# One block for attention, output products, routing and experts: semaphores in place of two barriers

## What is computed

```python
qkv = (x @ Wqkv + bqkv).reshape(B, L, 3, n_heads, head_dim)      # B, L, D = 2, 2048, 256
scores = q . k / sqrt(head_dim) + slopes * -|pos_q - pos_k|
x = layernorm(x + softmax(scores) @ v @ Wout + bout)
weights = softmax(x @ router_w.T + router_b)                      # 4096 tokens, 8 experts
top two of each token; expert e takes its first 512 tokens
y = sum over the picks of weight * relu(x @ w_in[e]) @ w_out[e]   # hidden width 1024
out = layernorm(x + y + weight_of_noop * x)
```

## Time and profile before

| | us |
|---|---|
| median of 3 runs | 1118.37 |
| lowest and highest of them | 1116.06, 1119.56 |
| the profiled execution | 1116.07 |
| its span, first to last instruction | 1114.3 |

### The profile page before, as it was taken

One profiled execution on the slowest core, in us unless ns is written; L12 is line 12 of the kernel. 1 busy time (PEld: TensorE's weight loads), 2 busy tenths in 40 slices (PEclk: granted clock), 3 DMA queues, 4 the chain that ended last, 5 costly groups with the idle time before them and its releaser, 6 DMA issues. The chain is left out here.

```text
span 1114.3 us, 35264 instructions
## 1 busy us (share of the span) xinstructions
PE 1045.0 (94%) x15370; PEld 659.1 (59%) x15370; DVE 436.9 (39%) x1016; ACT 824.7 (74%) x832; POOL 305.0 (27%) x454
## 2 busy tenths in 40 slices
PE   7999899999999999999899999999969469999996
PEld 4555566456576564675555766746447326666665
DVE  4778333453243222235334623323345721111163
ACT  3564799999999999999799999999955255111154
POOL 2333022122112111112221521211311073645433
PEclk9999899999999999999999999999999679999999
DMA  4765312221221121113222121210206246444473
GB/s 156 223 199 166 110 48 81 63 61 55 73 56 40 50 63 34 47 39 117 70 79 54 50 73 50 57 57 16 82 13 228 76 116 193 119 110 114 114 271 126
DMA packets 76506, 104.51 MB, mean 94 GB/s; under 512 B 13742, under 2 KB 62524, under 8 KB 76348
## 3 DMA queue, kind: packets, MB, share of 16 engines
q1 hardware_dynamic: 65708, 87.94, 25.4%
q0 software_dynamic: 6080, 9.06, 3.9%
q10 hardware_dynamic: 4560, 5.19, 1.4%
HBM read 66.49 MB, written 31.48 MB: 88 GB/s over the span
## 5 line engine op out<-in xcount | busy, mean ns | idle before, releaser
L975 ACT ACTIVATE prob<-ps 128x1536 f32<-128x1536 f32 (+4 forms) x504 | 667.3, 1460 | 38.1 <-PE ps L931 36.5
L931 PE MATMUL ps<-q_stack,k_stack 111*32 111x512 bf16 (+17 forms) x6848 | 431.3, 311 | 15.3 <-ACT prob L975 7.7
L955 PE MATMUL ps<-prob,v_head 128*32 128x128 f32 (+7 forms) x7228 | 431.4, 340 | 0.0
L931 PEld LDWEIGHTS ps<-q_stack,k_stack 111*32 111x32 bf16 (+5 forms) x6848 | 216.5, 97 | 202.1 <-ACT prob L975 112.8
L955 PEld LDWEIGHTS ps<-prob,v_head 128*32 128x32 f32 x7228 | 243.8, 110 | 78.2 <-issue 17.3
L986 POOL TENSOR_TENSOR prob<-prob,near_bias 128x128 f32<-128x128 f32 x256 | 125.9, 496 | 549.3 <-ACT prob L975 549.0
L986 DVE TENSOR_TENSOR prob<-prob,near_bias 128x128 f32<-128x128 f32 x256 | 86.3, 344 | 447.0 <-ACT prob L975 446.7
L1004 DVE RECIPROCAL o_rec<-o_den 128x128 f32<-128x128 f32 x128 | 112.9, 922 | 0.6
L1671 PE MATMUL ps<-xeT,w 128*128 128x512 f32 x224 | 99.1, 600 | 0.8 <-ACT xeT L1703 0.7
L1685 PE MATMUL ps<-w,hT 128*128 128x256 f32 x448 | 97.9, 379 | 0.0
L1749 ACT ACTIVATE hT<-ps 128x512 f32<-128x512 f32 x28 | 16.7, 596 | 108.1 <-PE ps L1671 107.9
(11 more groups left out here) (166 smaller groups left out, 598.3 us busy)
## 6 DMA issues: line engine op xcount, KB each, us to landing
qk_parts<-split SPq DMA_DIRECT2D x32, 384.0 KB, 2.8
w<-L_ffn_experts_inter_dram SPq DMA_DIRECT2D x7, 1024.0 KB, 6.1
w<-n_L_ffn_experts_out_dram SPq DMA_DIRECT2D x7, 1024.0 KB, 9.4
q_stack<-qk_parts SPq DMA_DIRECT2D x31, 192.0 KB
k_stack<-qk_parts SPq DMA_DIRECT2D x31, 192.0 KB
z_rows<-v SPq DMA_DIRECT2D x8, 516.0 KB, 3.4
xin<-in_L_attn_x_dram ACTq DMA_DIRECT2D x8, 512.0 KB, 5.0
heads<-o_out SPq DMA_DIRECT2D x128, 32.0 KB, 2.3
```

What stands on the lines that cost most here:

```text
L931: mm = pe.matmul(ps[k:k + keys, SLOT_BANKS * (c % 2) + bank, col:col + z - a], k_st[n % STACKS][0:rows, kb * P + k:kb * P + k + keys], q_s ...
L955: mm = pe.matmul(ps[32 * g:32 * g + 32, 6 + n % 2, column:column + width * times], vh[n % 2][:, kb, :], moving, start=g not in begun, stop ...
L975: act.activation(prob[:, c % RING, 0:at + z - a], ps[:, bank:bank + SLOT_BANKS, :].rearrange("p c n -> p (c n)")[:, 0:at + z - a], ACT.Exp ...
```

## The change

The four stages keep their work, their tiles and nearly all of their instructions. Three of them, attention, route and experts, no longer open a block: `attention_programs`, `route_programs` and `expert_programs` return one function for each engine, and `build` calls the three one after the other inside one block. With the blocks two barriers go, and these waits and signals come:

- PE waits for `heads_ready` before each group of products (1 for batch 0, 2 for batch 1), and before group 1 for `values_taken`. SP raises `heads_ready` at item 19 (behind a wait for the stores of the 16 items of batch 0) and at its end; DVE raises `values_taken` at the end of its attention list, behind a wait for `o_read`.
- SP waits for the first group of products before it loads the experts' weights, POOL before it makes the constants.
- POOL waits for `lot_step` and `z_out` before its first gather.
- The semaphores of the x loads are one for each group of 512 tokens from the first stage on, so that the counts waited for rise by 16.
- The last sums share `heads`' place in SBUF, and four tiles of the division are allocated outside of attention.

The diff without changes of indentation:

```diff
-def attention_phase(nc, t, x, parts_dram, shift_dram, heads_dram, q_pos, k_pos, ps):
+def attention_programs(nc, ctx, t, x, parts_dram, shift_dram, heads_dram, q_pos, k_pos, ps):
...
-            pool.wait_ge(x_in[c], 16)
+        pool.wait_ge(x_in[c], 32)
...
             if n == H + STACKS:
                 sp.wait_ge(vh_done, H)
                 load_rows(sp, 0)
+                for buf in range(2):
+                    sp.wait_ge(o_stored[buf], 16 * GROUPS * (H // 2))
+                sp.sem_inc(t["heads_ready"], 1)
...
         for buf in range(2):
             sp.wait_ge(o_stored[buf], 16 * GROUPS * (len(ITEMS) // 2))
+        sp.sem_inc(t["heads_ready"], 1)
...
                 else:
                     invert(n, step - INVERT)
+        dve.wait_ge(o_read, len(ITEMS))
+        dve.sem_inc(t["values_taken"], 1)
...
-        with nc.Block() as block:
-            @block.sync
-            def _(sp):
+    def sync(sp):
         bounded = sp.value_load(t["bounded"][0:1, 0:1], min_val=0, max_val=1)
         with sp.If(bounded == 1):
             banded_sync(sp)
         with sp.Else():
             general_sync(sp)
...
+    return sync, tensor, scalar, vector, gpsimd
...
-def route_phase(nc, t, w1_dram, w2_dram, z_dram, ps):
+def route_programs(nc, ctx, t, w1_dram, w2_dram, z_dram, ps):
...
-        block = ctx.enter_context(nc.Block())
...
+    def sync(sp):
+        sp.wait_ge(y_mm, 1)
         for par in range(2):
             load_expert(sp, t, w1_dram, w2_dram, par, par)
...
+    def tensor(pe):
         for n in range(NCH):
+            pe.wait_ge(t["heads_ready"], n // QG + 1)
+            if n == 1:
+                pe.wait_ge(t["values_taken"], 1)
             if n >= 2:
                 pe.wait_ge(z_done, n - 1)
                 pe.wait_ge(extra_done, n - 1)
...
+    def gpsimd(pool):
+        pool.wait_ge(y_mm, 1)
         prefix_weights(pool, earlier, ones, const)
...
-        sums = sb("sums", [P, NT, D], F32)
+    sums = t["heads"][:, :, :].rearrange("p k (t n) -> p (k t) n", n=D)
...
-        with nc.Block(no_gpsimd_drain=True) as block:
...
+        pool.wait_ge(t["lot_step"], 4)
+        pool.wait_ge(t["z_out"], 16 * NCH)
         for e in range(2):
             gather(e)
...
+        with nc.Block(no_gpsimd_drain=True) as block:
...
+            @block.tensor
+            def _(pe):
+                attend[1](pe)
+                route[1](pe)
+                experts[1](pe)
...
```

More of the change, by code:

```diff
@@ L358, in project_phase @@
         extra_done = sem("extra_done")
-        x_in = [sem(f"x_in{p}") for p in range(2)]
+        x_in = t["x_in"]
         scaled = sem("scaled")
@@ L437, in transposes @@
             def transposes(c):
-                pe.wait_ge(x_in[c % 2], (c // 2 + 1) * 16)
+                pe.wait_ge(x_in[c], 16)
                 if c >= 1:
@@ new lines, in pv @@
+                        mm = pe.matmul(ps[32 * g:32 * g + 32, 6 + b, :], vh[b][:, kb, :],
+                                       prob[:, ch % RING, c * CH:(c + 1) * CH],
+                                       start=(kb == 0), stop=(kb == KB - 1))
+                    mm.then_inc(pv_done, 1)
+                for ch in range(CHUNKS):
+                    score(ch)
+                    for kb in range(blocks_done(ch - PV_LAG - 1), blocks_done(ch - PV_LAG)):
+                        pv(kb)
+                for kb in range(blocks_done(CHUNKS - 1 - PV_LAG), KB):
+                    pv(kb)
@@ new lines, in general_gpsimd @@
+    def general_gpsimd(pool):
+        pool.sem_inc(vh_done, 2)
+        with pool.Fori(0, H) as h:
+            for b in range(B):
+                pool.wait_ge(pv_done, h * (2 * KB) + (b + 1) * KB)
+                pool.tensor_copy(vh[b][:, :, 0:HD], t["v"][:, b * KB:(b + 1) * KB, bass.ds(h * HD, HD)])\
+                    .then_inc(vh_done, 1)
+        for c in range(NCH):
+            add_bias(pool, c)
+    def sync(sp):
+        bounded = sp.value_load(t["bounded"][0:1, 0:1], min_val=0, max_val=1)
+        with sp.If(bounded == 1):
+            banded_sync(sp)
+        with sp.Else():
+            general_sync(sp)
@@ L2036, in build @@
         t["heads"] = ctx.enter_context(nc.sbuf_tensor("heads", [P, 2, T], F32))
+        for name in ("o_sum", "o_out"):
+            t[name] = [ctx.enter_context(nc.sbuf_tensor(f"{name}{b}", [P, CH], F32)) for b in range(B)]
+        for name in ("o_den", "o_rec"):
+            t[name] = ctx.enter_context(nc.sbuf_tensor(name, [P, CH], F32))
+        for name in ("heads_ready", "values_taken", "lot_step", "z_out"):
+            t[name] = ctx.enter_context(nc.semaphore(name))
         t["x_in"] = [ctx.enter_context(nc.semaphore(f"rows_in{c}")) for c in range(NCH)]
```

2079 lines of the change are left out of this document (1028 added, 1051 removed).

## The result

| | us |
|---|---|
| kernel before, median of 4 runs (lowest, highest) | 1117.92 (1116.06, 1119.56) |
| changed kernel, median of 4 runs (lowest, highest) | 1107.84 (1107.19, 1110.11) |
| ratio, 95% interval | 0.9914 [0.9893, 0.9935] |
| the profiled execution after, its span | 1110.11, 1108.4 |
| forecast | 1108.8 [1105.0, 1113.5] |

A forecast was written before the change was run, and what follows sets the result against it. PE bounds attention and experts, left alone; the gain lies between them, where PE waits 10.86 us at a barrier. 10.1 - 1.8 + 0.5 - 0.1 = 8.7 us less, from a mean of 1117.5: 1108.8 us, range 1105 to 1113.5.

The forecast's parts named there:

- The jump stays in the gap: Between attention and products, PE still jumps over the general program (3774 ns), so the first product comes 2.8 us after the last value.
- the other reading in the forecast: At PE's jump, a branch of about 108 ns would start the first product at 826.6, 0.8 us better overall.
- Eight groups at 3.58 us: Output products behind attention: eight groups at full clock take 28.6 us, ending at 857.9 against 868.03, 10.1 us earlier.
- The clock: Soon after PE restarts behind attention, half clock for 3.4 to 3.7 us costs 1.8 us; bounds 0 and 3.4.
- The rival with 0.27: The clock doesn't fall after PE's short stop behind attention; gain 10.5 us, time 1107.0 us; chance 0.27.
- No wait in the barrier's place: In the products, new waits don't stop PE; rival: late DVE or longer half clock, 1.5 to 3.5 us more, chance 0.13.
- the four margins: Signals for product groups 2 to 5 come before PE asks; for example, group 3's addition has 0.8 us to spare.
- The gather: Before the experts, POOL's first gather follows DVE by semaphore, 0.86 us instead of 1.35; gain 0.5, bounds 0 and 1.35.
- SP at item 19: In attention, SP's two added waits and a signal between the x reload and the next stacks cost 0.1 us.
- The rows' stores: Route stage stores share DMA with weight loads but land before the gather, with 14 us of cover.
- the rival of a gain given back: Late landing of the rows' stores holds the gather and eats the whole gain; 1117 us, chance 0.05.
- The stretch of the experts as long as before: In the profile after, the experts' stretch and the tail keep their length; no gain or loss there.

The follow-up runs named there:

- Experiment 8: Changed kernel with PE's eight groups of products and DVE's first two additions written ahead of their jump over the general program; 1108.30 us, 0.9897 of the kernel before.
- experiment 1: The changed kernel run again, unaltered; 1111.27 us against 1118.76 for the kernel before, ratio 0.9946.
- experiments 3: Changed kernel with the experts in their own block again, so the second barrier back and the first gone; 1110.41 us, 0.9927 of the kernel before.
- experiment 10: The changed kernel, unchanged, as the measure for kernels run beside it; 1110.15 us, 0.9937 of the kernel before.
- experiment 11: Changed kernel with the heads' sums and results back behind attention's other tiles, so at the old addresses; 1110.91 us, 0.9931 of the kernel before.
- experiment 4: Kernel before with eight unused products added to PE's list between its jump and the first barrier; 1117.17 us, ratio 0.9994.
- experiment 2: Changed kernel with attention in its own block again, so the first barrier back and the second still gone; 1120.99 us, 1.0022 of the kernel before.
- experiment 12: Changed kernel with PE's products and DVE's first two additions ahead of their jumps and the old addresses; 1107.62 us, 0.9906 of the kernel before.
- experiment 6: The kernel before, unchanged, run against itself; ratio 1.001.
- experiment 5: Changed kernel with both barriers back, its new waits, order of starts and addresses kept; 1121.21 us, 1.0012 of the kernel before.

## Why the prediction was right, point by point

- **The jump stays in the gap.** Forecast: first product 2.8 us behind the last value, 829.3, behind the branch and not a semaphore. Measured 2.79 us, 829.56, "issue", branch of 3.85 us. Experiment 8 shows that it is the jump: with the same work ahead of it the stop is gone. The row of before was the right term; the other reading in the forecast had the first product at 826.6, and in every trace with the products behind the jump they start 2.45 us or more behind the last value. (That reading was the Trainium skill's figure for a compare-and-branch, Advanced Engine Details and Errata, Control Flow Timing; the row of 3.85 us disagrees with it.)
- **Eight groups at 3.58 us.** Right: DVE's additions from group 2 on are 3.57 to 3.58 us apart. The hole of 0.51 us was missing, so the products ended at 859.24, inside the forecast's 857.9 to 859.7, but by another sum: 829.56 and 29.7 of products with the hole at full clock, not 829.3 and 28.6 + 1.8. That this end falls into the range is luck.
- **The clock: the step that failed as put.** "So I expect half clock for one stretch" came true for the products in one of five traces with a stop of 2.45 to 2.83 us (experiment 1); in the trace of after, in experiments 3, 10 and 11 the clock stayed at 1.00. With experiment 4, where it fell behind a stop of 2.31 us, it is two of six. The rival with 0.27 was the commoner case. The size was right: 30.56 us with the fall against 28.88 in experiment 4 and 29.0 in experiment 8 without. The row that I leaned on, the stop between projection and attention of 2.80 us, does not decide it: that stop was followed by half clock in all fourteen traces, the new one in one of five.
- **No wait in the barrier's place.** Right: PE waits in no group; the four margins held.
- **The gather.** 0.93 us instead of 1.35: 0.42 against the forecast's 0.5. Experiment 3 gives 0.52.
- **SP at item 19.** PE's stop nearest to it was 3.47 us at 533.82, one at another place than before (3.64 at 543.06). Over the fourteen traces such stops take 1.2 to 4.3 us, and attention takes 708.7 us against 709.0: no cost seen. The 0.1 us is below what can be told.
- **The rows' stores.** The forecast's cover was ample, but one statement was off: "lands in 3.3 us (5.3 at most)". Issued among the loads of the weights they take longer:

```profile
L1329 SPq DMA_DIRECT2D z_rows<-v x8: 359/902/5768, 840.1 to 863.8; - x8
...
DMA to landing us min/median/max: 3.6/7.9/13.7
```

The last of them, issued at 863.8, landed within 3.6 us all the same, some 15 us ahead of the gather, so the rival of a gain given back there is out.
- **"The stretch of the experts as long as before".** Wrong in this trace by 2.9 us. There is no late takeover in it; the clock does it. It was at half until 899.6, 5.7 us into the first expert (before 3.0), and once more from 913.3 to 916.7, behind a wait of 1.51 us for the second expert's rows that stands in the trace of before too, without a fall:

```profile
893.85:899.50 5.65, 5.65 (x7) 2.52 (x8) 0.00 (x0) 1.83 (x4) 4.43 (x5) 0.50 0.13 26
...
913.30:916.50 3.20, 3.05 (x11) 2.54 (x11) 0.00 (x0) 2.38 (x6) 0.00 (x0) 0.50 0.25 85
```

That is 1.4 + 1.7 us. The other three executions of after, 1107.19 to 1107.95, took 2 to 3 us less than this one.
- **The size of the whole.** Forecast 8.7 us, a ratio of 0.992. The three comparisons gave 0.9914, 0.9946 and 0.9937; 9.6, 6.0 and 7.0 us of 1118, so the forecast lies among them and 1.7 above their middle. That the first of them came within 1.0 us is in part luck, since the clock's 1.8 us mostly did not come and the hole and the experts, which the sum had at nothing, did. The first barrier gave 8.5 by the ratios and 9.7 by the medians (experiments 1 and 2 on one chip) against 8.3 forecast with the fall and 10.1 without. What lies between that and the whole is the rest of the change, which cost nothing in the sum: the two kernels with the first barrier back stand 1.3 and 2.5 us above the kernel before by their ratios. That this is real is not certain, since the kernel before against itself shows 1.1 us.
- **Two slips in the sum.** The "mean of all four times", 1117.5, counts the profiled execution twice, since 1116.06 and 1116.07 are the same one; the mean of the three is 1118.0, and the forecast by the same rule 1109.3. The lower end takes off 11.1 us where its own terms give 10.1 + 1.35 - 0.1 = 11.35, so 1104.7. Neither changes what follows.

## What to carry to other kernels

Look at the sequencer's own rows before you remove a barrier: what the engine does to get to its next work, here a jump over a long program of 3.4 to 3.9 us, stays when the wait goes, and sets the gain. Work that can go ahead of such a jump should be written there, if the engine waits for others afterwards; it gave another 3.3 us here (1107.62 against 1110.91 with the same addresses on one chip, 2.8 by the ratios; the intervals overlap, the traces show 3.2 us up to the last product), and the two versions with it have the lowest ratios of this study, 0.9897 and 0.9906. And a gain that is read from one trace of each kernel is as good as the spread of that kernel's other stretches: of the 9.1 us gained up to the last product, the one trace of after showed 3.1 given back, mostly by the clock.

## What the runs showed of the hardware

- PE's compare-and-branch into the program that follows it takes 84 to 88 ns in all fourteen traces. The one that jumps over the general program took 3.37 to 3.89 us in twelve, and 6.77 and 6.71 us in experiments 8 and 12, where it stands behind the products. It ended 1.41 to 1.51 us behind the landing of a 16 KB load of instructions in each. On DVE 2.29 to 2.54 us pass between the last scaling and the first instruction behind the jump (six traces without the first barrier).
- Stops of PE of 2.31 to 2.83 us behind the same work were followed by half clock in two executions of six. A stop of 5.12 us was followed by products of which 6.1 us were at half clock, stops of 10.8 to 11.1 us by 2.9 to 6.1 us, and with the last 8.8 us of such a stop filled by matmuls by none.
- From DVE's last write to POOL's first gather it took 0.93 us by a semaphore in eight traces, 1.35 to 1.36 through the end of a block in the four with the order of before, 1.44 to 1.45 in experiments 3 and 5.
- Stores issued among 4 MB of loads landed after 7.9 us in the median and up to 13.7, where they had landed after 3.3 and up to 5.3.
- In the first expert DVE's or ACT's takeovers came 1.1 to 3.7 us late, before PE itself had to wait, in eleven of fourteen traces (experiment 6, a short one, with 1.1 us among them, and the trace of after not), without a cause that the trace shows.
